# Attention and a product-key FFN on one core: TensorE's steps of the attention in another order

## The reference

```
qkv = x @ W_qkv.T + b_qkv                       # x is (4, 1024, 128), 16 heads of 8
scores = einsum('bhqd,bhkd->bhqk', Q, K) / sqrt(8)      # causal: keys after the query are -inf
attn = softmax(scores, axis=-1)
O = einsum('bhqk,bhkd->bhqd', attn, V)
out = O @ W_o.T + b_o
```

## Time and profile before

| | us |
|---|---|
| median of 3 runs | 861.89 (860.15 to 862.83) |
| profiled execution, time | 859.2 |
| its span, first to last instruction | 857.6 |
| TensorE busy | 739.3 (86%) |
| VectorE busy | 683.2 (80%) |
| ScalarE busy | 567.2 (66%) |
| GpSimd busy | 423.4 (49%) |

### The profile page before, as it was taken

The page is one execution under the profiler, slowest core; times in us unless marked ns, Lnnn a source line. Parts: engine busy times, 40 slices in busy tenths (PEclk is TensorE's granted clock), DMA queues, the critical chain, the costliest instruction groups (busy, mean ns, idle before and its releaser), DMA issues. The chain is left out here.

```text
span 857.6 us, 17568 instructions
## 1 busy us (share of the span) xinstructions
PE 739.3 (86%) x4345; PEld 323.0 (38%) x4345; DVE 683.2 (80%) x2289; ACT 567.2 (66%) x926; POOL 423.4 (49%) x468
## 2 busy tenths in 40 slices
PE   6758999999999999999999998696788888887755
PEld 4432233333332333233323331243456555554345
DVE  5669999898988898898889881156788888888883
ACT  4440267666766676667666767558889797897881
POOL 8655112221222112211222122267899999999984
PEclk9875699999999999999999999987999999999997
DMA  6757535335533653364336331201001101100000
GB/s 174 226 152 198 114 71 132 76 93 116 128 76 84 125 120 75 81 137 116 86 74 137 82 68 33 90 2 52 1 0 38 38 1 37 38 1 13 1 14 25
DMA packets 58955, 67.06 MB, mean 78 GB/s; under 512 B 15488, under 2 KB 33536, under 8 KB 58880
## 3 DMA queue, kind: packets, MB, share of 16 engines
q1 hardware_dynamic: 53120, 62.35, 30.5%
q10 hardware_dynamic: 5184, 2.36, 1.0%
q0 software_dynamic: 576, 1.57, 0.7%
HBM read 46.73 MB, written 19.53 MB: 77 GB/s over the span
## 5 line engine op out<-in xcount | busy, mean ns | idle before, releaser
L697 ACT ACTIVATE probs<-ps 128x384 f32<-128x384 f32 (+2 forms) x384 | 291.9, 810 | 174.4 <-PE ps L751 123.4
L668 POOL TENSOR_SCALAR_AFFINE_SELECT probs<-probs 128x256 f32<-128x256 f32 x256 | 102.9, 407 | 368.6 <-ACT probs L697 366.3
L807 DVE CUSTOM_DVE_ANT_0 junk<-ps,tri 128x256 bf16<-128x256 f32 (+3 forms) x512 | 229.1, 488 | 43.7 <-PE ps L719 36.0
L719 PE MATMUL ps<-Kx,Qx 128*128 128x512 bf16 (+3 forms) x768 | 230.8, 345 | 11.3 <-DVE mx L811 4.1
L751 PE MATMUL ps<-Qa,Ka 128*128 128x512 bf16 (+3 forms) x768 | 185.9, 328 | 15.0 <-DMA Qa<-m_scr 10.1
L737 PE MATMUL ps<-probs,Vg 128*9 128x512 f32 (+3 forms) x1536 | 159.3, 488 | 1.0 <-ACT Os L682 0.5
L811 DVE TENSOR_REDUCE mx<-ps 128x1 f32<-128x512 f32 x256 | 158.2, 679 | 0.3 <-DVE Vg L794 0.2
L719 PEld LDWEIGHTS ps<-Kx,Qx 128*128 128x128 bf16 x768 | 68.7, 97 | 204.4 <-DVE mx L807 124.8
L966 POOL TENSOR_TENSOR S<-sim 128x1024 f32<-128x1024 f32 x64 | 120.6, 1907 | 12.1 <-DVE A L1218 6.5
L1218 DVE SCALAR_TENSOR_TENSOR A<-S,T,ps 128x511 f32<-128x511 f32 x128 | 90.2, 741 | 11.3 <-ACT ps L1040 10.3
L751 PEld LDWEIGHTS ps<-Qa,Ka 128*128 128x128 bf16 x768 | 61.5, 97 | 90.8 <-ACT probs L697 44.3
(11 more groups left out here) (115 smaller groups left out, 868.5 us busy)
## 6 DMA issues: line engine op xcount, KB each, us to landing
Qx<-q_scr SPq DMA_DIRECT2D x48, 192.0 KB
Kx<-k_scr SPq DMA_DIRECT2D x48, 192.0 KB
Qa<-q_scr SPq DMA_DIRECT2D x48, 192.0 KB
Ka<-k_scr SPq DMA_DIRECT2D x48, 192.0 KB
o_scr<-Os SPq DMA_DIRECT2D x32, 256.0 KB, 2.1
q_scr<-qs SPq DMA_DIRECT2D x34, 128.0 KB, 3.3
k_scr<-qs SPq DMA_DIRECT2D x18, 128.0 KB, 3.3
xin<-in_L_attn_x_dram ACTq DMA_DIRECT2D x8, 256.0 KB, 3.7
```

Of the source, the lines that this page charges most:

```text
L668: pool.affine_select(out=diag, in_=diag, compare_op=ALU.is_ge, fill=0.0, base=0, pattern=[[0, 2], [1, P]], channel_multiplier=-1).then_inc ...
L697: act.activation(probs[:, k % 2, hh, 0:width], ps[:, bank:bank + 2, :].rearrange("p a c -> p (a c)")[:, 0:width], ACT.Exp, scale=SM_SCALE) ...
L719: pe.matmul(ps[:, X_BANK + f % X_SLOTS, 0:c1 - c0], Qx[:, u, hh, P * i:P * (i + 1)], Kx[:, u, hh, c0:c1], start=True, stop=True).then_inc( ...
L807: dve.tensor_tensor_reduce(out=junk[:, f % 4, 0:w], in0=src, in1=tri[:, CHUNK - w:CHUNK], scale=1.0, scalar=-BIG, op0=ALU.add, op1=ALU.max ...
```

## The change

```diff
-AHEAD = 20
+AHEAD = 18
-GROUP_ORDER = "psxxxpxxsxxsxsxpxspxxsxxpxxxspxxssxxsxpxsxxxsxpxxxsxspsxxsxpxxsxsxxsxpxxsxpxsxsxsxsx"
+GROUP_ORDER = "xpxxpxsxxsxxsxxsxppxxsxsxxpxxxsspxxsxsxppxxsxxsxxxxxsspxsxxsxpxxsxsxpxssxxxpsxsxxsxs"
 CARRIED = 4
 COPY_AT = (12, 4)
 X_SLOTS = 3
+VG_AT = 41
...
                     def group(n, u, last):
                         for f in range(CPG):
-                            if f == 12 and last < 2:
+                            if f == VG_AT and last < 2:
                                 dve.wait_ge(pv_done, PPG * n + PV_START)
                                 dve.tensor_copy(Vg[:, 1 - u, :, :, :], vaug[:, bass.ds(n + 1, 1), :, :, :].rearrange(
```

## The result

Over runs taken in turn, the changed kernel takes 853.75 us (median of 4, 851.66 to 854.91) and the kernel before 862.36 us (median of 4). The ratio is 0.9902, 95% interval 0.9875 to 0.9929: faster by 1.0%. Forecast was 853.5. The profiled execution took 851.7 us with a span of 850.1, against 859.2 and 857.6 before; each is as fast as the fastest timed run of its kernel or faster, and 7.5 us lie between the two traces and 8.6 between the medians. That the forecast was met to 0.25 us is luck: the runs of one kernel lie 3 us apart.

What follows compares the result with a forecast made beforehand. The maxima's chain was taken to bound the groups, with the hand-over of max chunks taking over. Saving 7.6 us in 14 groups plus 0.5 at the ends, 8.1, gave 853.8, said as 853.5; range 849 to 859.

Steps and rivals of the forecast that it cites:

- the edges: Turns of DVE's loop, every second group: 2.45 us between chunks instead of 0.60, 1.85 lost, which the order can't remove.
- the chain: Row maxima from half 0's copy through store, loads, write and reads to next first scores; sets old groups, 28.2 us.
- the hand-over: Max chunks passing from PE to DVE through three banks; starves DVE and becomes the bound after the change.
- Term (b): First scores after two products and four chunks: 1.5 us later in the group, hiding the chain's last part.
- Term (c): AHEAD 18: two chunks move from prologue to second last group; 0 to 1.2 us gained, counted with the ends.
- Term (e): New order's runs walked: 27.98 us a group, 28.2 with allowances against 28.74, saving 7.6 over 14 groups.
- Term (a): Two pairs of products per group: 0.21 us of PE saved each, 0.42 a group, useful only where PE is late.
- Term (d): Vg's copy after 41 chunks instead of 12: neither gain nor loss, within 0.3 us a group.
- The ends: Shorter prologue, second last group and last group, where pairs and scores lie under ScalarE: 0.5 us gained together.
- (1): Rival: the chain stays the bound, its DMA part stretching 0.8 us; gain 4 us, 858; chance 0.14.
- (2): Rival: the walk holds without allowances, 27.98 us a group; gain 12 us, 850; chance 0.13.
- (5): Rival: masks come too late for the second pair; 0.85 us late costs 4 us, 866; chance 0.06.

Runs made afterwards that it cites:

- e11: Kernel before, with DVE's stream written out without a loop: 859.1 us, ratio 0.996.
- e12: Kernel before, with DVE's stream written out and the maxima's write and reads issued ahead of the six Qx and Kx loads: 846.7 us, ratio 0.981.
- e5: Kernel before, with only the first scores of a group put later, behind the second product and its chunk: 862.1 us, ratio 1.001.
- e1: Kernel before, with the maxima's write and reads issued ahead of the six Qx and Kx loads: 865.7 us, ratio 1.006.
- e6: Changed kernel, with the first scores of a group put back ahead of the second product: 865.3 us, ratio 1.0035.
- e9: Changed kernel, with DVE's stream written out without a loop and the maxima's write and reads ahead of the six loads: 839.8 us, ratio 0.973 to the kernel before.
- e8: Changed kernel, with DVE's copy of V back ahead of chunk step 12: 854.0 us, ratio 0.991 to the kernel before.
- e3: Changed kernel, with the two pairs of products drawn apart: 851.7 us, ratio 0.989 to the kernel before.
- e10: As e9, with the two pairs of products also drawn apart: 842.3 us, ratio 0.976 to the kernel before.
- e7: Changed kernel, with DVE's loop written out over all groups: 842.8 us, ratio 0.978 to the kernel before.
- e2: Changed kernel, with the maxima's write and reads issued ahead of the six Qx and Kx loads: 872.8 us, ratio 1.013 to the kernel before.

## Why the prediction was right, point by point

- **What bounds the kernel before: shown, with a second bound just under it.** With the edges gone but the chain there the old order takes 28.67 a group, and 27.70 when the chain goes too (e11, e12). TensorE waited for the chain in front of every steady group's first scores, and the edges lay under it: removing them gave 0.15 a group. Right under it was the hand-over with its edges, 28.83 in e5, which the prediction didn't work out for the old order. e1 by itself couldn't show this, since it made the edges longer. One reading was wrong: the granted clock wasn't 2.4 GHz through the whole stage. From 66 to 100 us, ahead of the first scores, it was 1.2 GHz, as the 5 and the 6 in the earlier trace rows say; the groups that the sum counts aren't touched.
- **Term (b), first scores later: its mechanism right, its account incomplete.** It is necessary (e6: 11.6 us) and not sufficient (e5: 0). The forecast had it so, the hand-over being the bound that is left; what it didn't price was that without the cover the new order would be slower than the old one. The chain itself was sized right: the copy ends 13.5 to 13.8 us behind the first scores, 13.9 was said.
- **Term (c), two chunks fewer ahead: not seen.** From the first max chunk to the first scores it is 37.5 us where it was 36.5: the two chunks left the prologue, but four now stand in front of the first scores, and the clock stood at 1.2 GHz for 41 us there against 34. `AHEAD` wasn't changed by itself.
- **Term (e), the walk: right, a little short.** It gave DVE's first chunk of a group 26.87 us behind that of the group before without an edge between them, 27.0 in the trace (268.82 to 295.82), and 29.05 with one, 29.5 in the trace (to 325.32). With the allowances 28.2 a group, 28.26 measured. Without them it was 0.3 a group short, and e9 shows that these 0.3 are in the hand-over (27.3 for 27.05): the 0.1 that was added for the chain's variation was needed elsewhere, which is luck. What in the change, beyond cover and pairs, shortens the hand-over wasn't tried apart; by e8's trace V's copy may have a part in it.
- **Term (a), the pairs: failed.** The steps are as worked out (0.23 where 0.21 was said; the second product 0.44 us behind a first one of 256 columns), but they are worth nothing in the steady groups of this kernel (e3), and 0.16 a group at most where nothing else binds (e10). PE's busy time, for which 0.3 less was forecast, stayed at 27.5 a group. Behind a pair TensorE waits for DVE's banks anyway; that this is the reason follows from the walk and was not tried by itself. The sum didn't suffer, since the walk ran over DVE's time. The Trainium skill's rule (TensorE: Matmul & The Clock Gate, What happens when you issue a matmul), by which a weight load is pulled ahead of running matmuls, would, as the prediction drew from it, make a pair save no time of TensorE at all; this trace doesn't agree with that, the 0.23 us are there.
- **Term (d):** within the 0.3 a group that was said; by the traces of e8 the copy's new place may be worth 0.25, by the medians nothing.
- **The edge: right, and more than was said of it.** "The order can't take that away" holds; the loop can, and in the changed kernel, unlike in the one before, it pays: 11.0 against 3.3 us on the medians, 8.7 against 1.3 in the 13 groups of the traces. The changed order uncovered the edge.
- **The ends and the sum.** 7.5 us between the profiled spans, 8.6 between the medians; forecast 8.1. The parts were off against each other. Between the first scores of the second group and of the second last it is 5.9 us less in 13 groups (0.45 each, where 0.54 was said for 14). But first scores are a moving mark here, for they stand later in the new order. Counted from the first carried product of each group, which stands at nearly the same place, the 13 groups give 6.2 us (0.48 each), the second last 0.6 and the last, to the end of its last product, 1.15, and the stretch ahead of them costs 0.5. So the steady groups were put 1.4 us too high and the ends, 0.5 said and some 1.2 measured, too low. In the last group no chunks are made and TensorE's waits are mostly for ScalarE's exponentials. Without x the old order reads psps..., the new one ppssss...: more scores stand ready in front of a product that waits for exponentials or masks. e9 and e12 show the same 1.2; which place of the order gives it wasn't tried.
- **Rivals.** (1), the chain as the bound, didn't happen, but it lies right behind: it takes over in some groups once the edges are gone (e7), and is worth 3 to 4 us there (e9). (2), the walk without allowances: 0.3 a group too short, as said. (3), a switch without a price of its own: the price is in the timeline (e3). (5), late masks: TensorE's matmuls never waited for one in the steady groups, only four weight loads did, 0.2 us each; GpSimd was done 0.98 us before the second pair's start, 0.76 was said.

## What to carry to other kernels

Where two limits close a loop at the same time, taking one away measures next to nothing (e5, e11), and an edit that takes it away may even look harmful by a side effect (e1, e2): remove both, then put them back one by one. An order of steps is worth its time only if it keeps the slowest consumer fed; steps saved on an engine that then waits for a buffer can be worth nothing, however well they are measured (e3). When a loop's edge shows as idle "issue", write the loop out or give it more work per turn, and keep large loads away from the moment of the branch.

## What the runs showed of the hardware that was not expected

- The time at a loop's edge depends on the DMA traffic. DVE's step from the last chunk to the first behind the branch was 2.46 to 2.8 us (2.95 once) where the DMA engines were nearly idle (share 0.03 to 0.12 in the step), 3.5 to 4.3 in e1 and 4.3 to 5.2 in e2, where loads were in flight (share 0.8 in the 2 us before). The 8 KB instruction packet that lies ahead of the branch otherwise came only when the loads were nearly through, and the next one took 1.03 us, where 0.3 to 0.6 is usual. TensorE's own loop of two groups showed no such gap: 0.28 us from its branch to the next instruction.
- A stall of DVE can cost TensorE its clock: in e2 TensorE was idle for 2.8 us at an edge, and the granted clock was 0.50 for the next 3.4 us. Behind one edge of six it did not fall.
- DVE's stream without a loop, some 14 groups long, had one idle time of "issue" in eight groups, 0.3 us (e7).
